# Second weights loaded in the norms, a new order of TensorE's work in two self attentions, and unread products at a loop's head

## The reference

```python
x = x + L0_xattn(ctx, layernorm(x))      # attention of x on itself and on 77 context rows, 8 heads of 64
x = x + L0_ffn(layernorm(x))             # 8 experts; the experts choose rows
x = x + L1_xattn(layernorm(x), ctx)      # cross attention, 16 heads of 16
x = x + L1_ffn(layernorm(x))             # self attention, 16 heads of 16, then 8 experts, 2 for a row
x = x + L2_xattn(layernorm(x), ctx)
x = x + L2_ffn(layernorm(x))             # 8 experts, 2 for a row
x = x + L3_xattn(layernorm(x), ctx)
x = x + L3_ffn(layernorm(x))             # 4-bit rounded feed forward
```

```python
scores = einsum('bqhd,bkhd->bhqk', q, k) / sqrt(16)
o = einsum('bhqk,bkhd->bqhd', softmax(scores, axis=-1), v)
```

## Time and profile before

| | us |
|---|---|
| median of 3 runs | 2773.51 |
| lowest and highest run | 2765.41, 2776.91 |
| profiled execution | 2775.61 |
| its span | 2773.8 |
| TensorE busy, share of the span | 2197.8, 79% |
| VectorE busy | 1285.1, 46% |
| ScalarE busy | 1088.8, 39% |
| GpSimd busy | 650.5, 23% |
| mean granted TensorE clock | 0.884 |

### The profile page before, as it was taken

How to read it: one execution, slowest core, us unless ns; L and a number is a source line. 1 busy time by engine, 2 the same in 40 slices (tenths; PEclk the granted TensorE clock), 3 DMA queues, 4 the chain that set the end, 5 groups by cost and what they waited for, 6 DMA issues and landing times. The chain is left out here.

```text
span 2773.8 us, 36374 instructions
## 1 busy us (share of the span) xinstructions
PE 2197.8 (79%) x12198; PEld 1298.8 (47%) x12199; DVE 1285.1 (46%) x2559; ACT 1088.8 (39%) x2189; POOL 650.5 (23%) x569
## 2 busy tenths in 40 slices
PE   4899999961958865999998279994954999858687
PEld 2433333241943431333334179993334999823354
DVE  4654444146035448678861410004443350154895
ACT  2524444420423511567675144442522444425111
POOL 0238888821420050000000022220001222110011
PEclk8989999985977985799999589997986999978798
DMA  1000000021620035223320466662035666410000
GB/s 62 1 5 9 13 13 13 21 69 48 211 84 1 1 135 61 31 32 50 44 32 6 153 203 204 196 201 88 3 122 175 197 203 198 136 42 1 0 1 31
DMA packets 141630, 214.34 MB, mean 77 GB/s; under 512 B 39600, under 2 KB 97644, under 8 KB 141500
## 3 DMA queue, kind: packets, MB, share of 16 engines
q1 hardware_dynamic: 131804, 186.17, 24.6%
q0 software_dynamic: 9696, 26.49, 2.5%
HBM read 182.00 MB, written 30.15 MB: 76 GB/s over the span
## 5 line engine op out<-in xcount | busy, mean ns | idle before, releaser
L2873 PE MATMUL experts_up_ps<-experts_rowT,experts_w 128*128 128x128 f32 x2864 | 341.0, 277 | 0.0
L1805 DVE TENSOR_REDUCE heads_part_max<-heads_shared_ps 128x2 f32<-128x1024 f32 x256 | 300.1, 1221 | 85.4 <-PE heads_shared_ps L1722 85.4
L1789 ACT ACTIVATE heads_probs<-heads_score_ps 128x512 f32<-128x512 f32 x512 | 266.4, 602 | 186.3 <-PE heads_score_ps L1744 186.3
L2873 PEld LDWEIGHTS experts_up_ps<-experts_rowT,experts_w 128*128 128x128 f32 x2864 | 333.0, 194 | 0.2
L1323 POOL TENSOR_TENSOR core_xT<-core_xT,heads_probs 128x1024 f32<-128x1024 f32 (+1 forms) x112 | 264.5, 2362 | 32.4 <-ACT heads_probs L1492 20.4
L3028 DVE TENSOR_TENSOR experts_y<-experts_down_ps,experts_b_now 128x256 f32<-128x256 f32 x78 | 33.1, 425 | 498.0 <-PE experts_down_ps L2883 497.9
L2936 ACT ACTIVATE experts_hT<-experts_up_ps,experts_b_now 128x128 f32<-128x128 f32 x624 | 223.1, 368 | 47.5 <-PE experts_up_ps L2873 10.4
L1531 DVE TENSOR_REDUCE heads_part_max<-heads_shared_ps 128x1 f32<-128x512 f32 x256 | 164.6, 686 | 153.3 <-PE heads_shared_ps L1365 153.2
L1744 PE MATMUL heads_score_ps<-heads_q,heads_k 66*128 66x512 f32 x512 | 195.4, 468 | 30.2 <-ACT heads_probs L1789 26.0
L2822 POOL DMA_INDIRECT y_dram<-experts_y,experts_index x101 | 99.4, 984 | 455.8 <-DVE experts_y L3028 411.1
L1492 ACT ACTIVATE heads_probs<-heads_score_ps 128x1024 f32<-128x1024 f32 x128 | 131.1, 1024 | 186.7 <-PE heads_score_ps L1392 173.0
(11 more groups left out here) (541 smaller groups left out, 3208.0 us busy)
## 6 DMA issues: line engine op xcount, KB each, us to landing
experts_w<-in_L_ffn_W SPq DMA_DIRECT2D x39, 1024.0 KB, 5.2
experts_w<-in_L_ffn_w SPq DMA_DIRECT2D x39, 1024.0 KB, 5.2
experts_w<-in_L_ffn_W SPq DMA_DIRECT2D x23, 512.0 KB
experts_w<-y_dram SPq DMA_DIRECT2D x20, 512.0 KB, 4.9
experts_b_now<-in_L_ffn_b SPq DMA_DIRECT2D x78, 128.0 KB, 2.9
heads_q<-l_queries SPq DMA_DIRECT2D x32, 256.0 KB, 12.2
heads_k<-l_keys SPq DMA_DIRECT2D x32, 256.0 KB, 13.8
l1f_w<-in_L_ffn_W SPq DMA_DIRECT2D x8, 1024.0 KB, 11.8
```

The lines of the kernel that those rows point to most:

```text
L1789: act.activation(probs[:, t % SLOTS_OF_PROBS, r, :], score_ps[:, i % RING, :], ACT.Exp, scale=SC).then_inc(exp_done, 1)
L1805: dve.tensor_reduce(part_max[:, g % 2, 2 * pair:2 * pair + 2, s, x], two, AX.X, ALU.max).then_inc(shared_read, 1)
L2873: done = pe.matmul(up_ps[:, f % 4, 0:SLOT], w1_sb[:, u, c, f * P:(f + 1) * P], rowT[:, u % 2, c, :], start=(c == 0), stop=(c == DC - 1))
```

## The change

1. **Second weights.** The block of their own is gone. `layer_norm` and `gate` take `second_weights`; SyncE issues all eight transfers in the norm of the first expert stage, and five in the norm and three in the gate of the two others. The loads of the gate's weights and bias, and those of the expert stage's columns and first bias, move from SyncE's list to the head of ScalarE's.
2. **heads1.** The fourth score comes behind the two PEAK items. Ahead of step 0 stand 18 products of `q_narrow` with itself into `sums_ps` that nobody reads, and five more in each of the steps 0 and 1; before `value(0)` TensorE waits until they have ended.
3. **heads0.** The PEAK items of a step come ahead of its score; in `work_at` they also come ahead of a WEIGH of the same step.

```diff
@@ layer_norm
-        if gain is not None:
-            @block.sync
-            def _(sp):
+        @block.sync
+        def _(sp):
+            if gain is not None:
                 sp.dma_start(affine[:, 0, :], column(gain, DC)).then_inc(loaded, 16)
                 sp.dma_start(affine[:, 1, :], column(shift, DC)).then_inc(loaded, 16)
+            if second_weights is not None:
+                second_weights.begin(sp)
@@ gate, sync
-            if transposed:
-                sp.dma_start(w_raw[:], w).then_inc(loaded, 16)
-            else:
-                sp.wait_ge(w_cleared, 1)
-                sp.dma_start(w_sb[:, :, 0:E], chunked(w)).then_inc(loaded, 16)
-            if bias is not None:
-                sp.dma_start(bias_sb[:], across(bias, E)).then_inc(loaded, 16)
+            if second_weights is not None:
+                second_weights.go_on(sp)
             sp.wait_ge(loaded, 32 if bias is not None else 16)
@@ gate, scalar
+            if transposed:
+                act.dma_start(w_raw[:], w).then_inc(loaded, 16)
+            else:
+                act.wait_ge(w_cleared, 1)
+                act.dma_start(w_sb[:, :, 0:E], chunked(w)).then_inc(loaded, 16)
+            if bias is not None:
+                act.dma_start(bias_sb[:], across(bias, E)).then_inc(loaded, 16)
@@ pair_attention
-        if s in WEIGH_AT and 0 <= HALVES * g + WEIGH_AT[s] - (s == 3) * HALVES < HALVES * PAIRS:
-            work_at[t].append((WEIGH, HALVES * g + WEIGH_AT[s] - (s == 3) * HALVES))
         if t < STEPS:
             work_at[t] += left[0:2]
             left = left[2:]
+        if s in WEIGH_AT and 0 <= HALVES * g + WEIGH_AT[s] - (s == 3) * HALVES < HALVES * PAIRS:
+            work_at[t].append((WEIGH, HALVES * g + WEIGH_AT[s] - (s == 3) * HALVES))
...
             for t in range(STEPS):
+                for item in work_at[t]:
+                    if item[0] == PEAK:
+                        share(item)
                 score(t)
                 for item in work_at[t]:
-                    share(item)
+                    if item[0] != PEAK:
+                        share(item)
                 if t:
                     value(t - 1)
@@ quad_attention
+        BEFORE, EARLY = 18, 2
...
+            def keep_running(times):
+
+                for _ in range(times):
+                    pe.matmul(sums_ps[:], q_narrow[:, 0, 0:P], q_narrow[:, 0, 0:512], start=True,
+                              stop=True).then_inc(rested, 1)
+
             for item in work_at[-1]:
                 share(item)
+            keep_running(BEFORE)
             for t in range(STEPS):
                 items = work_at[t]
-                for r in range(QUAD):
+                early = t < EARLY
+                for r in range(QUAD - 1):
                     score(t, r)
+                    if early:
+                        keep_running(1)
                 for item in items[0:2]:
                     share(item)
+                    if early:
+                        keep_running(1)
+                score(t, QUAD - 1)
+                if t == 1:
+                    pe.wait_ge(rested, BEFORE + EARLY * (QUAD + 1))
                 if t:
                     value(t - 1)
@@ SecondWeights
-    def begin(self, nc, name, w2):
-        with Stage(nc, name) as st:
-            block = st.block()
-
-            @block.sync
-            def _(sp):
-                for e in range(E):
-                    sp.dma_start(self.sb[:, e, :, :], w2[e].rearrange("(c p) d -> p c d", p=P)).then_inc(self.loaded, 16)
+    def load(self, sp, experts):
+        for e in experts:
+            sp.dma_start(self.sb[:, e, :, :], self.w2[e].rearrange("(c p) d -> p c d", p=P)).then_inc(self.loaded, 16)
+
+    def begin(self, sp):
+        self.load(sp, range(0, self.in_norm))
+
+    def go_on(self, sp):
+        self.load(sp, range(self.in_norm, E))
@@ sparse_experts, sync
-            if affine is not None:
-                for x in range(2):
-                    sp.dma_start(columns[:, x, :], column(affine[x], DC)).then_inc(const_loaded, 16)
             if has_bias:
-
-                sp.dma_start(b1_raw[:], b1).then_inc(b1_out, 16)
                 sp.wait_ge(b1_copied, 1)
@@ sparse_experts, scalar
+            if has_bias:
+                act.dma_start(b1_raw[:], b1).then_inc(b1_out, 16)
+            if affine is not None:
+                for x in range(2):
+                    act.dma_start(columns[:, x, :], column(affine[x], DC)).then_inc(const_loaded, 16)
@@ build
-                second = SecondWeights(keep, 4 * D)
-                second.begin(nc, "w2of1", a["L1_ffn_W2"])
-                layer_norm(nc, core, "ln1g", rows_out=hats, gain=a["L1_ffn_ln2_g"], shift=a["L1_ffn_ln2_b"], source=rows)
+                second = SecondWeights(keep, 4 * D, a["L1_ffn_W2"], 5)
+                layer_norm(nc, core, "ln1g", rows_out=hats, gain=a["L1_ffn_ln2_g"], shift=a["L1_ffn_ln2_b"], source=rows,
+                           second_weights=second)
```

More of the change, by code:

```diff
@@ L819, in __init__, with gate @@
         self.top = stage.sb("top", [P, choices, NT])
-def gate(nc, core, name, routing, w, transposed, bias, kind, probs_out=None):
+def gate(nc, core, name, routing, w, transposed, bias, kind, probs_out=None, second_weights=None):
     SIDE = P // 4
@@ L3078, in build @@
                 rows = moe.sb("rows", [P, NT, D])
-                second = SecondWeights(moe, 2 * D)
-                second.begin(nc, "w2of0", a["L0_ffn_W2"])
-                layer_norm(nc, core, "ln0f", rows_out=rows)
+                second = SecondWeights(moe, 2 * D, a["L0_ffn_W2"], E)
+                layer_norm(nc, core, "ln0f", rows_out=rows, second_weights=second)
                 routing = Routing(moe, 1)
@@ L3119, in build @@
                     routing = Routing(moe, 2)
-                    gate(nc, core, "gate1", routing, a["L1_ffn_gate_w"], False, a["L1_ffn_gate_b"], "pair_softmax")
+                    gate(nc, core, "gate1", routing, a["L1_ffn_gate_w"], False, a["L1_ffn_gate_b"], "pair_softmax",
+                         second_weights=second)
                     sparse_experts(nc, core, "experts1", routing, hats, 4 * D,
@@ L3133, in build @@
                 rows = moe.sb("rows", [P, NT, D])
-                second = SecondWeights(moe, 4 * D)
-                second.begin(nc, "w2of2", a["L2_ffn_w2"])
-                layer_norm(nc, core, "ln2f", rows_out=rows)
+                second = SecondWeights(moe, 4 * D, a["L2_ffn_w2"], 5)
+                layer_norm(nc, core, "ln2f", rows_out=rows, second_weights=second)
                 routing = Routing(moe, 2)
-                gate(nc, core, "gate2", routing, a["L2_ffn_gate_w"], True, a["L2_ffn_gate_b"], "pair_probs")
+                gate(nc, core, "gate2", routing, a["L2_ffn_gate_w"], True, a["L2_ffn_gate_b"], "pair_probs",
+                     second_weights=second)
                 sparse_experts(nc, core, "experts2", routing, rows, 4 * D,
```

6 lines of the change are left out of this document (4 added, 2 removed).

## The result

| | before | after |
|---|---|---|
| median, us | 2771.3 (4 runs, 2765.4 to 2776.9) | 2700.0 (4 runs, 2700.0 to 2704.6) |
| span of the profiled execution, us | 2773.8 | 2698.3 |
| TensorE busy, us | 2197.8 | 2183.5 |
| mean granted clock | 0.884 | 0.892 |

The ratio is 0.9747, 95% interval 0.9723 to 0.9771. The forecast was 2701 us. That closeness is partly luck: two terms were wrong by 13.0 and 9.8 us, in opposite directions. Ratios here and in the table of experiments leave out two slow executions, one of the kernel before beside e3, e4, e5 and e8 (3819 us, mean clock 0.567) and the longest of f2 (2716.7 us).

What follows compares the result with a forecast made beforehand. No engine was taken to bound the whole program; each stage ends on its own wait. 44.6 + 0.4 - 2 + 18.9 + 11.4 + 0 = 73.3 us less, written as 2701 us; range 2686 to 2722.

Steps and rivals of the forecast that it cites:

- Second weights: Three expert stages: the wait for the block of eight issues before each norm goes whole, 44.6 us less.
- follow-on wait for gain and shift: Second expert stage's norm: gain and shift now stand ahead of the weights, so ScalarE waits less, 0.4 us.
- Gates: Gate stages: small loads on ScalarE's queue beside second weights cost 1 us at each of two gates; range 0 to 12.
- the prediction's own sign of being wrong: Gate stages: a DMA wait of over 5 us ahead of the gate's products would show the forecast wrong.
- The bound from rows: Gate loads queued behind their own ring: at most two 1.0 MB loads of some 3 us, 6 us a gate.
- the penalty near the low end: Gate loads: with DMA engines taking turns packet by packet, the penalty is near the low end, sum within 2 us.
- First self attention: heads0, values, maxima, scores in another cycle: nothing removed or hidden, 0 us; range -6 to +12 us.
- Rival three: heads0: the maxima's load behind the values lies open, 0.10 or 0.18 us a step, 2713 to 2723 us; chance 0.08.
- Fourth score: heads1, steps 10 to 107: maxima fill the fourth score's wait, 2.70 us a step, 18.9 us less.
- Unread products: Head of heads1: they lift the clock about halfway; first score 2.3 us late, 11.4 us gained in all.
- Rival two: Head of heads1: clock stays at 0.50 or falls again in step 2, a loss of 9.6 us, 2722; chance 0.08.
- Clock elsewhere: Later stages: clock flips counted only in the forecast's own spread, 2690 to 2712 us, with no term.

Runs made afterwards that it cites:

- e3: Kernel after, but in the second self attention the fourth score again stands behind the third, ahead of the maxima; 2718.7 us.
- e4: Kernel after without any of the 28 unread products and without the wait for them; 2718.9 us.
- e5: Kernel after with the 18 unread products ahead of the loop and none in its steps 0 and 1; 2697.8 us.
- e8: Kernel after, but SyncE loads the gate's weights and bias at the head of the norm before, ahead of the second weights; 2680.9 us.
- f2: Kernel after with the gate's loads ahead of the second weights, 12 unread products ahead of the loop, none in steps 0 and 1; 2690.8 us.
- e1: Kernel after with the second weights in a block of their own again, the gate's small loads staying on ScalarE; 2735.3 us.
- e2: Kernel after, but in the gate SyncE issues its three second weights only when the gate's own two loads have landed; 2698.8 us.
- e7: Kernel after, but in the first self attention the maxima products stand between the max rows' products and the score products; 2712.7 us.
- f3: Kernel after, but from the third group of heads VectorE reads 256 of 512 columns of each maxima product in the second self attention; 2689.1 us.

## Why the prediction was right, and where it was wrong

- **Second weights, right.** 44.35 us of blocks went, by the three rows that the sum took; 44.6 was forecast, and the named follow-on wait for gain and shift went too (0.26 us, where 0.4 was its term).
- **Gates, the step that failed by its size.** The prediction took 1 us for each of two gates, from the row of a scatter beside megabyte loads (3.1 us to landing), and kept 12 as the other bound. The waits grew by 4.75 and 3.64 us, 8.4 in all; norms and gates that ran longer at half clock bring the stretch to 11.4 (the third norm's products took 6.64 us instead of 5.76, the first gate's 3.34 instead of 2.72), and that part had no term. More than a DMA wait of 5 us ahead of the gate's products was the prediction's own sign of being wrong, and it came. e1 and e2 show the cause: with the 1 MB loads out of the way the wait is gone (e1) or nearly so (e2). The scatter's row was the low one of its view. The same view of the kernel before, transfers from 1610 to 1900 us, has the gather on the same queue:

```profile
y_dram<-experts_y,experts_index POOLq DMA_INDIRECT x39, 3.1
experts_row<-rows_dram,experts_index POOLq DMA_INDIRECT x35, 6.7
```

Taken from the gather, 6.7 us in place of 3.15, the term would have been some 3.6 us a gate, 7 in all, close to the 8.4 measured. The DMA engines are also less busy there, 0.58 of the time against 0.89 while the small loads of the second gate moved. The bound from rows, at most two transfers' time (6 us), held. The Trainium skill ("DMA: Bandwidth & Descriptors", "Queues, rings and completion order") has the DMA engines take turns between queues packet by packet. The trace agrees as far as packets of both queues pass side by side, 1213 and 416 of them; but the penalty near the low end that was drawn from it had the wrong size, 4.8 us beside three large transfers. Of these, 2.2 us lie ahead of the first small packet, and what holds it back there is open.
- **First self attention, the step that failed by its sign.** "What may move is which weight load is hidden" was the right question. The error was to look at the load that becomes exposed (0.10 us) without the one it replaces, that of the float32 max rows, which had been exposed all along at 0.18 to 0.19 us. e7 shows the difference: some 0.1 us in each of the 121 steps with maxima. WEIGH's own move, 0.2 us in 13 of them, was not costed at all. First to last exponential is 355.2 us against 368.9, so the term is -13.6 us, outside the range of -6 to +12 of that term; 0.6 us that the loop began later bring the stretch to -13.0. Rival three fell with it.
- **Fourth score, right.** Forecast 2.70 us a step by VectorE's period, measured 2.74; 18.9 us, measured 18.4 from step 10 to the end. f3 shows that VectorE is what holds it above 2.64, and e3 that the order is what brought it.
- **Unread products, right in sign and cause, larger in worth.** The first score came 1.6 us late (forecast 2.3), steps 0 to 9 took 29.4 us (forecast 30.9) against 44.6, and the clock rose after ten of the 18, about halfway, as assumed. (With nine at 0.43 us and nine at half of that the prediction's own numbers give 1.6 us late and not 2.3.) That is 13.6 us, where 11.4 was the term. Without the unread products the clock came even later than in the kernel before (e4's trace), so beside the new order they carry about 20 us. Rival two fell. Its counter-argument, that they use all 128 rows and columns, is not shown: no run gave unread products of another shape.
- **Clock elsewhere.** Untouched stages moved by -4.4 and +7.1 us. The forecast had this in its range only.

The failed terms, -13.0 against 0 and +11.4 against +1.6, cancel to 3.2 us. That they did is luck.

## What to carry to other kernels

Take the loads of the next stage out of a block of their own, but issue the small ones first: a small load that someone waits for took two to three times as long here when megabytes were issued beside it, and cost nothing when it went ahead of them (e8). When TensorE is the bound, try the order of a step's products in which the shortest weight load comes behind the products that use all rows; it was worth 0.1 us a step here. Unread products at the head of a loop can be worth many times their time (1.6 us of delay for about 20 us), but the count may need a margin: measure several executions, not one trace. And take the price of a load from all rows of its kind in the view, not from the lowest.

## What was not expected of the hardware

- A gate's loads of 8 KB and less took 7.9 us to the first product beside three 1 MB loads and 3.1 alone (second stage; after, e1), and 4.2 beside the tail of five where it is 2.9 alone (third stage; e2, e1).
- Half clock under unbroken work: 61.4 busy of 62 us at 0.50 in e4, on a loop that then ran on at 1.00 to its end; with 18 products of 128x128 ahead, in after, the clock was up after 4.5 us of them.
- With 12 in place of 18 the same program took either 2671 to 2676 or 2706 to 2717 us (f2, six executions).
